# Attention stage of a two-block MetaFormer kernel: the feature map as one maximum on VectorE, the squared mean subtracted by TensorE, the squares of x3 on GpSimd

## The reference, cut to what matters

```python
def _L1_conv_ref(x, ...):                  # x: channel-normalized x2
    q = einsum('oc,bchw->bohw', q_w, x) + q_b
    Q = elu(q) + 1.0                       # the feature map; K likewise, on a 4x subsample
    Z = 1.0 / (einsum('nlhd,nhd->nlh', Q, K.sum(axis=1)) + EPS)
    out = einsum('nlhd,nhdv,nlh->nlhv', Q, KV, Z) * S
    return einsum('oc,bchw->bohw', proj_w, out) + proj_b
x3 = x2 + _L1_conv_ref(_ln_c(x2), ...)     # _ln_c: mean and variance over 64 channels
t  = x3 + experts(_ln_t(x3))               # logits of 32 experts, softmax over tokens, top 8
```

## Time and profile before

| | |
|---|---|
| median of 3 runs | 2014.13 us (2013.77 to 2014.66) |
| the profiled execution | 2016.03 us, span in the trace 2014.2 us |
| PE, DVE, ACT, POOL busy | 77%, 73%, 63%, 71% of the span |
| the attention stage | about 1177 to 1793 us of the span |
| DMA | 429.87 MB, 213 GB/s |

### The profile page before, as it was taken

One profiled execution on the slowest core, in us unless ns is written; L12 is line 12 of the kernel. 1 busy time (PEld: TensorE's weight loads), 2 busy tenths in 40 slices (PEclk: granted clock), 3 DMA queues, 4 the chain that ended last, 5 costly groups with the idle time before them and its releaser, 6 DMA issues. The chain is left out here.

```text
span 2014.2 us, 24846 instructions
## 1 busy us (share of the span) xinstructions
PE 1559.5 (77%) x5690; PEld 654.7 (33%) x5690; DVE 1472.8 (73%) x2369; ACT 1268.0 (63%) x2235; POOL 1435.8 (71%) x1066
## 2 busy tenths in 40 slices
PE   4999999999999962976681669999999999935200
PEld 1333333333333311654451332232332323204200
DVE  1789999999999862995686547999999999952000
ACT  3777777777777622975671348898888988820000
POOL 3999999999999940155685219988889888901571
PEclk8999999999999985987886789999999999965555
DMA  5578888888887658588986247878888887661011
GB/s 156 173 226 250 246 254 236 255 256 238 255 250 223 185 178 234 172 313 292 346 302 250 105 138 229 266 268 273 271 260 259 264 272 251 204 156 25 2 2 1
DMA packets 121185, 429.87 MB, mean 213 GB/s; under 512 B 53424, under 2 KB 58448, under 8 KB 75984
## 3 DMA queue, kind: packets, MB, share of 16 engines
q1 hardware_dynamic: 99360, 423.81, 66.7%
q10 hardware_dynamic: 18736, 4.29, 1.4%
q0 software_dynamic: 2944, 0.18, 0.1%
HBM read 257.91 MB, written 170.01 MB: 212 GB/s over the span
## 5 line engine op out<-in xcount | busy, mean ns | idle before, releaser
L454 ACT ACTIVATE tap_products<-xn,kk 128x512 f32<-128x512 f32 x384 | 275.3, 718 | 164.2 <-POOL x_and_products L485 159.8
L485 POOL TENSOR_TENSOR x_and_products<-tap_products,x_and_products 128x512 f32<-128x512 f32 x256 | 326.6, 1276 | 41.5 <-POOL x_and_products L485 3.5
L385 PE MATMUL pst<-xn,taps 128*128 128x512 f32 x768 | 351.1, 592 | 0.0
L1426 POOL TENSOR_SCALAR exp_q<-exp_q 128x512 f32<-128x512 f32 x128 | 201.6, 1575 | 118.7 <-ACT exp_q L1381 118.7
L896 DVE SCALAR_TENSOR_TENSOR pss<-region,bn,pss 128x256 f32<-128x256 f32 x432 | 194.4, 489 | 85.3 <-PE pss L798 84.4
L833 POOL TENSOR_TENSOR x_block<-x_block,region 128x2048 f32<-128x2048 f32 x24 | 133.1, 5545 | 148.0 <-ACT region L820 81.6
L543 DVE SCALAR_TENSOR_TENSOR pst<-xn,kk,pst 128x512 f32<-128x512 f32 x256 | 192.5, 752 | 62.0 <-PE pst L385 61.8
L385 PEld LDWEIGHTS pst<-xn,taps 128*128 128x128 f32 x768 | 145.6, 190 | 186.2 <-issue 186.2
L485 POOL TENSOR_TENSOR x_and_products<-tap_products,x_ring 128x512 f32<-128x512 f32 x128 | 164.2, 1283 | 19.3 <-ACT tap_products L454 19.3
L1440 POOL TENSOR_TENSOR q_z<-q_map,z_inv 128x512 f32<-128x512 f32 x128 | 163.7, 1279 | 7.1 <-issue 5.3
L425 ACT ACTIVATE sq<-x_ring 128x512 f32<-128x512 f32 x256 | 157.6, 622 | 16.7 <-POOL x_ring L492 10.1
(11 more groups left out here) (236 smaller groups left out, 3044.4 us busy)
## 6 DMA issues: line engine op xcount, KB each, us to landing
rstd_wide<-rstd_scratch SPq DMA_DIRECT2D x128, 512.0 KB, 7.2
x_ring<-in_x SPq DMA_DIRECT2D x32, 1024.0 KB, 5.3
x_scratch<-x_ring SPq DMA_DIRECT2D x32, 1024.0 KB, 4.3
xl_scratch<-wx SPq DMA_DIRECT2D x32, 1024.0 KB, 8.7
region<-xl_scratch SPq DMA_DIRECT2D x32, 1024.0 KB, 10.5
x_ring<-x_scratch SPq DMA_DIRECT2D x32, 1024.0 KB, 8.5
rstd_of_channels<-rstd_scratch SPq DMA_DIRECT2D x64, 512.0 KB, 6.0
x_transposed<-x_squares SPq DMA_DIRECT2D x64, 512.0 KB, 5.0
```

Of the source, the lines that this page charges most:

```text
L385: m = pe.matmul(wide(pst[g % 2]), taps[:, n * P:(n + 1) * P], tap_rows(g, t), start=(n == 0), stop=(n == len(PE_TAPS) - 1))
L454: act.activation(prod[:, n, :, :], tap_rows(g, t), ACT.Copy, scale=kk[:, t:t + 1]).then_inc(products, 1)
L485: pool.tensor_tensor(xr[:, g % XR, :], prod[:, n, :, :].rearrange("p r w -> p (r w)"), xr[:, g % XR, :] if n else x_tile(g), ALU.add).then ...
L1426: pool.tensor_scalar(e, e, 1.0, None, ALU.min).then_inc(clipped, 1)
```

## The change

1. `map_query` becomes one DVE instruction, max(q + bias + 1, clipped exponential). POOL's sum (L1433) and DVE's `relu_query` (L1479) go. POOL still clips.
2. `variance` on DVE goes. Instead PE adds minus the identity times the squared mean to `ps_second`, as a fifth matmul, over all 128 columns of the array, after a wait for ACT's square of the mean.
3. `square_x3` moves from ACT to POOL, as a product of x3 with itself.
4. Rings and lags: the scaled query has 4 buffers (was 2), the exponential 4 (was 3), the map 4 (was 6); QSCALE is 8 (was 9), the map and denominator come at 10 (was 11), POOL's clip at 9 (was 11), product, attend and x3 at 12 (was 13), squares of x3 at 14 (was 13), transposes at 16 (was 14), the statistics of x3 at 17 (was 18), the gate at 20 (was 23) and its scaling at 22 (was 23). Within a step, PE now does the statistics ahead of the gate; the two now fall on different steps.

```diff
-            LOAD, SQ2, QUERY, QSCALE, QMAP, DENOM, BYZ, ATTEND, X3, SQ3, TURN = -6, 0, 7, 9, 11, 11, 13, 13, 13, 13, 14
-            STATS = (3, 18)
-            GATE, GSCALE, BEST, BEST_AT, EXPSUM = 23, 23, 25, 26, 29
+            LOAD, SQ2, QUERY, QSCALE, QMAP, DENOM, BYZ, ATTEND, X3, SQ3, TURN = -6, 0, 7, 8, 10, 10, 12, 12, 12, 14, 16
+            STATS = (3, 17)
+            QCLIP = 9
+            GATE, GSCALE, BEST, BEST_AT, EXPSUM = 20, 22, 25, 25, 28
...
@@ PE, stats_of
                     for j in range(TPB):
-                        m = pe.matmul(pse[32 * j:32 * j + 32, :], stat32[:, :], sq[l][:, (TPB * k + j) % SQSLOTS[l], :],
-                                      start=True, stop=True)
-                    m.then_inc(second_ready, 1)
+                        pe.matmul(pse[32 * j:32 * j + 32, :], stat32[:, :], sq[l][:, (TPB * k + j) % SQSLOTS[l], :],
+                                  start=True, stop=False, skip_group_check=True)
+                    pe.wait_ge(msq_done, n + 1)
+                    pe.matmul(pse[:, :], neg_ident[:, :], msq[:, :], start=False, stop=True, skip_group_check=True).then_inc(second_ready, 1)
...
@@ POOL
+                def square_x3(g):
+                    pool.wait_ge(x3_ready, g + 1)
+                    if g >= SQSLOTS[1]:
+                        pool.wait_ge(second_ready, round_of[1, (g - SQSLOTS[1]) // TPB] + 1)
+                    pool.tensor_tensor(sq[1][:, g % SQSLOTS[1], :], x_tile(g), x_tile(g), ALU.mult).then_inc(squared[1], 1)
...
@@ DVE, map_query
+                    dve.wait_ge(clipped, g + 1)
                     dve.wait_ge(q_scaled, g + 1)
...
-                    dve.tensor_scalar(qm[:, g % QSLOTS, :], qs[:, g % 2, :], qb, 0.0, ALU.add, ALU.max).then_inc(relu_ready, 1)
+                    dve.scalar_tensor_tensor(out=qm[:, g % QSLOTS, :], in0=qs[:, g % QRING, :], scalar=qb1[:, 0:1],
+                                             in1=eq[:, g % 4, :], op0=ALU.add, op1=ALU.max).then_inc(mapped, 1)
```

More of the change, by code:

```diff
@@ L1118, in build_program @@
             SLOTS = 8
-            QSLOTS = 6
+            QSLOTS = 4
+            QRING = 4
             TSLOTS = 3
@@ L1130, in build_program @@
             rstd = sb("rstd3", [P, 2, TILE], F32, ph)
-            qs = sb("query", [P, 2, TILE], F32, ph)
-            eq = sb("exp_q", [P, 3, TILE], F32, ph)
+            qs = sb("query", [P, QRING, TILE], F32, ph)
+            eq = sb("exp_q", [P, 4, TILE], F32, ph)
             qm = sb("q_map", [P, QSLOTS, TILE], F32, ph)
+            qb1 = sb("q_bias_plus_1", [P, 1], F32, ph)
+            neg_ident = sb("neg_ident", [P, P], F32, ph)
             lnd = sb("ln_d", [P, TILE], F32, ph)
@@ L1272, in _ @@
                         rstd_to_experts(k)
+                    if (h := pair_at(t, TURN + 1)) is not None:
+                        store_xt(h)
                 for k in range(NBLK - SEMS, NBLK):
@@ L1340, in _ @@
                             stats_of(l, k)
+                    if (p := pair_at(t, GATE)) is not None:
+                        gate(p)
             @blk.scalar
@@ L1378, in exp_query @@
                     act.wait_ge(q_scaled, g + 1)
-                    if g >= 3:
-                        act.wait_ge(mapped, g - 2)
-                    act.activation(eq[:, g % 3, :], qs[:, g % 2, :], ACT.Exp, bias=qb).then_inc(expq_ready, 1)
+                    if g >= 4:
+                        act.wait_ge(mapped, g - 3)
+                    act.activation(eq[:, g % 4, :], qs[:, g % QRING, :], ACT.Exp, bias=qb).then_inc(expq_ready, 1)
                 def log_denominator(g):
@@ L1409, in _ @@
                             rsqrt(l, k)
+                    if (g := tile_at(t, SQ2)) is not None:
+                        square_x2(g)
+                    if (k := block_at(t, EXPSUM)) is not None:
+                        exp_logits(k)
                     if (g := tile_at(t, QSCALE)) is not None:
@@ L1509, in best_logits_at @@
                     dve.tensor_scalar(nm[:, k:k + 1], cand[:, k * K:k * K + 1], -1.0, None, ALU.mult).then_inc(neg_ready, 1)
+                dve.tensor_scalar(qb1[:, :], qb, 1.0, None, ALU.add).then_inc(prepared, 1)
+                dve.tensor_scalar(neg_ident[:, :], ident, -1.0, None, ALU.mult).then_inc(prepared, 1)
+                dve.wait_ge(prepared, 2)
                 for t in range(0, STEPS_D):
-                    rounds = [(l, k) for l in range(2) if (k := block_at(t, STATS[l] + 1)) is not None]
+                    if (g := tile_at(t, QMAP)) is not None:
+                        map_query(g)
+                    if (k := block_at(t, BEST)) is not None:
+                        best_logits(k)
                     if (g := tile_at(t, QSCALE)) is not None:
@@ L1516, in _ @@
                         turn_x3(g)
+                    rounds = [(l, k) for l in range(2) if (k := block_at(t, STATS[l] + 1)) is not None]
+                    for l, k in rounds:
+                        clamp(l, k)
+                    if (k := block_at(t, BEST_AT)) is not None:
+                        best_logits_at(k)
+                    if (p := pair_at(t, GSCALE)) is not None:
+                        scale_logits(p)
                     if (g := tile_at(t, X3)) is not None:
                         add_attention(g)
-                    for l, k in rounds:
-                        variance(l, k)
-                    if (g := tile_at(t, QSCALE)) is not None:
-                        relu_query(g)
-                    for l, k in rounds:
-                        clamp(l, k)
-                    if (p := pair_at(t, GSCALE)) is not None:
-                        scale_logits(p)
-                    if (k := block_at(t, BEST_AT)) is not None:
-                        best_logits_at(k)
-                    if (k := block_at(t, BEST)) is not None:
-                        best_logits(k)
         with ExitStack() as ph:
```

58 lines of the change are left out of this document (17 added, 41 removed).

## The result

The changed kernel takes 2034.07 us, the median of 4 executions (2033.03 to 2036.18), against 2014.39 for the kernel before, measured beside it: a ratio of 1.0097, 95% interval 1.008 to 1.0115. The forecast was 2032 us in a range of 2009 to 2060, slower with a chance of 0.75. The profiled execution took 2033.25 us, with a span of 2031.5; the working made it "about 2034".

The account below looks back on a forecast made before the run. PE was taken to bound the changed kernel at 18.54 us a block; terms of -2.5, +18.5, +1 and +0.5 gave +17.5, with the wait +18, on the median of 2014.13: 2032 us, range 2009 to 2060.

Parts of the forecast that it names:

- price list: PE's matmul costs in the attention stage, switches included: steps of 5.59 and 3.68 us, 18.54 us a block, no wait.
- B: Rival: PE waits for ACT's square of the mean; 2068 us if all 1.33 us of waits survive, 2050 if half; chance 0.19.
- the 0.82: PE's wait in us for a scaled query of its own step, expected to go with the new lags.
- DVE's map: The new two-input operation per tile on DVE: 0.7 to 0.7 + 1.28 us, taken as 1.1, hidden under PE.
- C: Rival: DVE's map waits for a whole POOL product, 1.98 us, DVE needs 20 us a block: 2071 us; chance 0.04.
- D: Rival: PE's switching penalties come from just-in-time semaphores and vanish with looser lags, block 17.2 us: 1996 us; chance 0.13.
- E: Rival: part of PE's switching penalties vanishes or the start gains more, time within 0.2%: 2009 to 2018 us; chance 0.12.
- A product of the same shape: On POOL, x3's square replaces the sum of 1.27 us at equal cost: 4.13 us a tile again.
- start up to tile 8: Start of the attention stage until POOL's product of tile 8: at 1237.7 instead of 1240.21, -2.5 us.
- Tile 8 to 115: Steady stretch of 107 steps at PE's 4.635 us: 495.9 us instead of 477.4, +18.5.
- To tile 127: End stretch from tile 115, where POOL binds: 49.6 us at most for 47.6, less some overlap, +1.
- Behind it: After tile 127: x3's last square on POOL, 1.3 for 0.6, and the identity for the subtraction, +0.5 us.

Follow-up runs that it names:

- the first experiment: Changed kernel with the subtraction back on DVE (clamp after it) and no identity matmul: 2030.54 us, ratio 1.0081.
- the last kernel with the gate beside: Changed kernel without identity, subtraction on DVE, clamp on ACT, plus the gate on the statistics' steps and ahead of them: 1998.69 us, ratio 0.9914.
- 2029.78: Changed kernel, identity kept, with the gate moved onto the steps of the statistics and ahead of them: 2029.78 us, ratio 1.007.
- 2087.47: Changed kernel with minus half the identity added twice instead of minus the identity once: 2087.47 us, ratio 1.0353.

## Why the prediction was right, and where its terms were off

**The bound and the price list.** Right, and exact: steps of 5.59 and 3.68, 18.54 against 18.53 measured, no wait on PE. The list also gave the blocks of two other kernels to the hundredth (identity twice, and subtraction on DVE with the clamp on ACT). It is a floor, not a forecast, where another engine or a collision binds: 16.82 for 18.55 in the first experiment, 16.63 for 17.20 in the last kernel with the gate beside. The Trainium skill's 216 ns for a matmul of 512 columns ("TensorE: Matmul & The Clock Gate", Back-to-back issue gap) would have made the identity 0.22; the identity twice shows 0.86 again.

**The wait for the squared mean (B).** 0.12 us early was predicted, 0.12 was measured. B falls for this kernel. But its picture, waits that survive, is what the identity does on the old lags (1.18 of 1.33 us stay). The prediction saw only the end of the chain behind the 0.82, the scaling in the same step; it begins at the gate, and the changed kernel is rid of it because it scales the logits two steps behind the gate and takes the scaled query with another lag. Which of the two lags did it was not tried.

**DVE's map and the port (C).** I took 1.1 us, between 0.7 and 1.98; in the steady state it is 0.75, the lower end, and DVE needs 15.4 us a block, not 16.5. Nothing hung on it, since PE covered both. C falls for the time, while its mechanism is real: maps of 1.69 appeared as soon as PE's phase changed. The Trainium skill's rule ("GPSIMD Engine Reference", Key points) that GpSimd contends with VectorE's instructions of two SBUF inputs agrees with these maps, 0.74 undelayed and 1.69 behind a product. The traces add who pays, the one that starts second, and how much, 1.08 us less the offset behind a product; C's whole product of 1.28 was the upper end and a little too dear.

**POOL.** "A product of the same shape" was 0.23 us too dear (1.04 for 1.27), and the product beside the map came out at 1.36 for 1.28. At the start of the stage either the square (1.49) or the clip (1.93 for 1.48) of each tile was stretched, so that its 4.13 us a tile was right by errors that cancel: that is luck (from tile 8 to 12, 1238.54 to 1255.10, it took 4.14).

**Switching penalties (D, E).** Attend behind narrow weights still starts 0.96 apart, with looser lags; D and E fall. The penalties are PE's own.

**The sum.** The terms, predicted and measured: start up to tile 8, -2.5 and -1.7, from two errors that nearly cancel: tile 0 came at 1205.17 and not at 1207.2, and the two steps without squares took 3.19 and 5.31 us, not 2.86 each. Tile 8 to 115, +18.5 and +14.7: this is the mis-sized term. 107 steps at 4.635 assume that PE sets the pace from tile 8 on, but POOL, without a gap at 4.14 us a tile, does up to tile 13: tile 8 comes 2.85 us later than where PE's pace, counted back from tile 60, would have it, so there were 2.85 us fewer to go. Another 0.84 is the place of tile 115 within its block, where steps of 3.7 and 5.6 alternate. To tile 127, +1.0 and +1.1. Behind it, +0.5 and +2.2 to the last exponential of the logits (1809.52 against 1793.16, less the 14.17 us that product 127 came later); what makes that 1.7 more was not tried. Then +0.9 between there and the end of the span, for which I had nothing. Together +17.5 and +17.3. That the sum fits so well is partly luck: the long stretch was 3.8 us too dear, and the start and the end, some 3.5 us too cheap together, gave it back. The medians lie 19.7 us apart and not 17.3, because the profiled execution of the kernel before was 1.6 us above its median and that of the changed one 0.8 below.

**What the change is worth by parts.** Put into the kernel before by itself, the identity costs 47.9 us (2062.89 for 2014.99), and all the rest of the change gives 28.8 of them back (2034.07). Of the changed kernel's +19.7 us it is the cause in this sense too: without it, and with the clamp off DVE, the same kernel takes 1986.86. It is not so that taking the identity away is enough (2030.54). The change relieved PE of its 1.33 us of waits, filled it with 1.72 us of identity and 0.19 of an additional trip; what it took off the other three, read from the earlier trace rows and the same stretch after and scaled to a block (DVE 16.8 to 15.4 us, ACT 16.0 to 14.4, POOL 16.1 to 15.8), was hidden under PE.

**What stays open.** Why the phase of map and product falls one way in one kernel and the other way in the next was read from traces only; no run shifted it by itself. The size of the delay at a given offset is read from the traces too. What the lags alone do to the changed kernel can't be told from the one run that has them with the old work.

## What to carry to other kernels

Make the price list from start to start on the engine whose records overlap, count what each step issues with the switches, and compare it with the period of today: 1.9 us of work moved onto an engine that lacks only 1.3 us a block makes the block longer (0.57 us here) even if every wait on it goes, and where the waits stay nearly all of the work is paid (1.56 of 1.72 us on the old lags). A wait goes away only if its whole chain is loosened; follow it back through the queue of the engine that is waited for. When you take such work off again, look at what is next: here DVE was full within 2 us, and the gain appeared only with a second edit. And where two engines collide on their inputs, the one that starts second pays, the more the closer it starts behind the first, so that a kernel's time can hang on the phase between them.

## What the runs showed of the hardware

- A product on POOL of 128x512 fp32 takes 1.04 us with one buffer as both inputs and 1.27 to 1.28 with two.
- A map on DVE with two SBUF inputs takes 0.74 to 0.75 us undelayed. Right at or behind the start of POOL's product it takes up to 1.82, of its square up to 1.54, of its clip up to 1.15; it is delayed no longer if it starts 1.08, 0.84 or 0.41 us behind them. POOL's product right behind the map's start takes up to 1.84 (1.27 alone).
- A full-width fp32 matmul of 512 columns costs 0.86 us behind another and 0.96 behind narrow weights, in the changed kernel and in the kernels of 2062.89, 2029.78, 2087.47 and 1986.86 us alike, at a granted clock of 1.00.
- Behind a gap of 2.08 us on PE the granted clock of ten microseconds was 0.87, and matmuls took 1.50 and 1.70 us instead of 0.96 and 0.86; in the changed kernel, whose PE has no gaps, it stayed at 1.00 from 1400 to 1600 us.
